# Causal self-attention in a decoder kernel: three score units for two batches instead of four

## What is computed

```
q, k = rope(x @ wq), rope(x @ wk);  v = x @ wv          # 16 heads of 8
s = (q_h . k_h) / sqrt(8), -inf where key > query       # 128 x 128 per batch and head
x = layernorm(x + (softmax(s) @ v_h, heads joined) @ wo)
```

## Time and profile before

| | us |
|---|---|
| median of 3 runs | 1953.66 (1953.19 to 1954.66) |
| the profiled execution's own span | 1948.6 |
| what lies around the span (median minus span) | 5.1 |
| the self-attention block within the span | 0 to about 309.4 |
| one group in its middle, from `a_Y` to `a_Y` | 34.9 |

### The profile page before, as it was taken

One profiled execution on the slowest core, in us unless ns is written; L12 is line 12 of the kernel. 1 busy time (PEld: TensorE's weight loads), 2 busy tenths in 40 slices (PEclk: granted clock), 3 DMA queues, 4 the chain that ended last, 5 costly groups with the idle time before them and its releaser, 6 DMA issues. The chain is left out here.

```text
span 1948.6 us, 31799 instructions
## 1 busy us (share of the span) xinstructions
PE 1562.9 (80%) x10219; PEld 1017.4 (52%) x10219; DVE 1491.3 (77%) x2947; ACT 953.5 (49%) x1491; POOL 920.7 (47%) x938
## 2 busy tenths in 40 slices
PE   8889888989699978977878878769998811699991
PEld 4545547988476632322333333236776611588891
DVE  6899986887488779999989999967777678533335
ACT  3545543575544567657656666436566410011114
POOL 4455442444200147677676677654344100366653
PEclk8999998999899989999988999979999855799996
DMA  4000000000000000000000000020000040466654
GB/s 144 2 0 0 0 1 27 2 2 1 12 1 0 1 1 1 1 1 0 0 1 0 0 0 1 1 78 11 5 9 5 3 145 0 159 209 206 212 171 135
DMA packets 49075, 75.34 MB, mean 39 GB/s; under 512 B 8861, under 2 KB 34821, under 8 KB 48437
## 3 DMA queue, kind: packets, MB, share of 16 engines
q1 hardware_dynamic: 43541, 64.12, 10.5%
q0 software_dynamic: 4544, 9.32, 1.6%
q10 hardware_dynamic: 864, 0.33, 0.1%
HBM read 62.26 MB, written 11.48 MB: 38 GB/s over the span
## 5 line engine op out<-in xcount | busy, mean ns | idle before, releaser
L1506 POOL TENSOR_TENSOR m_hC<-m_h,m_Cs 128x512 f32<-128x512 f32 x256 | 328.2, 1287 | 169.2 <-DVE m_h L1680 122.6
L1788 PE MATMUL PS<-m_hC,identf 128*128 128x512 f32 x512 | 296.5, 662 | 100.9 <-POOL m_hC L1506 99.9
L1680 DVE TENSOR_TENSOR_SCAN m_h<-m_dA,PS 128x512 f32<-128x512 f32 x256 | 312.4, 1220 | 11.2
L1788 PEld LDWEIGHTS PS<-m_hC,identf 128*128 128x128 f32 x512 | 93.0, 203 | 236.4 <-POOL m_hC L1506 208.9
L1675 DVE TENSOR_TENSOR PS<-PS,m_DU 128x512 f32<-128x512 f32 x256 | 178.4, 697 | 19.9 <-issue 3.8
L1616 ACT ACTIVATE m_dA<-m_DT,m_A 128x508 f32<-128x508 f32 x256 | 174.3, 714 | 31.3 <-DVE m_DT L1664 31.1
L1996 ACT ACTIVATE e_Sg<-PS 128x512 f32<-128x512 f32 x71 | 42.4, 597 | 223.0 <-PE PS L2238 178.8
L2238 PE MATMUL PS<-e_xT,e_WT 128*128 128x128 f32 x1136 | 143.8, 281 | 4.9 <-DVE e_xT L2146 3.4
L1608 ACT COPY m_Cs<-PS 128x512 f32<-128x512 f32 x128 | 73.7, 576 | 143.7 <-PE PS L1766 143.5
L2238 PEld LDWEIGHTS PS<-e_xT,e_WT 128*128 128x128 f32 x1136 | 135.4, 195 | 9.3 <-DVE e_xT L2146 7.1
L1935 POOL DMA_INDIRECT e_XG<-token_rows,e_ids x71 | 68.8, 969 | 138.9 <-DVE e_ids L2140 117.6
(11 more groups left out here) (411 smaller groups left out, 3801.6 us busy)
## 6 DMA issues: line engine op xcount, KB each, us to landing
e_WT<-in_w_wgu SPq DMA_DIRECT2D x71, 512.0 KB
token_rows<-X SPq DMA_DIRECT2D x2, 2048.0 KB
e_Y<-expert_rows SPq DMA_DIRECT2D x16, 256.0 KB, 4.0
k_BD<-in_w_bcr SPq DMA_DIRECT2D x1, 2464.0 KB, 9.5
e_w_wd<-in_w_wd SPq DMA_DIRECT2D x1, 2048.0 KB, 7.9
out_dram<-X SPq DMA_DIRECT2D x8, 256.0 KB, 2.4
X<-in_x SPq DMA_DIRECT2D x1, 1792.0 KB, 8.7
x_Cs<-in_ctx SPq DMA_DIRECT2D x8, 154.0 KB
```

The lines of the kernel that those rows point to most:

```text
L1506: nc.gpsimd.tensor_tensor(hC[:, i % ND, :], hst[:, i % ND, :], Cs[:, n % ND, :], ALU.mult).then_inc(s["hC"], 1)
L1680: nc.vector.tensor_tensor_scan(hst[:, i % ND, :], dA[:, i % NA].rearrange("p b l -> p (b l)"), bank(4), 0.0, ALU.mult, ALU.add).then_inc(s ...
L1788: nc.tensor.matmul(bank(5 + ch), c.identf[:, :], hC[:, i % ND, :], start=False, stop=(n == NS - 1)).then_inc(s["yacc"], 1)
```

## The change

The self-attention gets a function of its own, `causal_attention`; `attention` stays for the cross call. Two batches (a **pair**, e = 0, 1) now share the 128 lanes: batch e has lanes 64e to 64e+63. A pair has UP = 3 units. Units 0 and 1 hold the queries 64 to 127 of both batches, 8 heads x 128 keys each. Unit 2 (EARLY) holds the queries 0 to 63 of both batches, 16 heads x 64 keys. So a group has UN = 6 units, each of the same 128 x 1024 elements as before. What follows from it:

- A late unit's scores are four matmuls with 64-column weights (two row groups x two column groups) of 512 columns, and the mask is 64 keys wide: two matmuls of 4 x 64 columns.
- An early unit is scored in two halves (`early_half`, `score_rest`), each four matmuls and two masks of 256 columns. The second waits for the first (semaphore `lo`) and stands one step later in PE's order.
- Outputs are made once a pair: for each batch 16 matmuls for the late and 8 for the early queries, all over 64 moving columns.
- The early queries need the values of keys 0 to 63 in another layout, `a_VL`: 8 more small matmuls a group (`project_early_values`), two more ACT copies of 64 partitions, and in the prelude a POOL memset of 128 x 3072.
- PE's stream is unrolled over the groups; the other engines keep the loop.

```diff
+    UP = 3
+    UN = PAIRS * UP
+    EARLY = 2
+    VL = sb("VL", [P, 2, GB * 4, VE])
...
+            def early_values(g, par, at=AUX):
+                act.wait_ge(s["ep"], g + 1)
+                for hp in (0, 1):
+                    r = slice(HQ * hp, HQ * hp + HQ)
+                    nc.scalar.copy(VL[r, par].rearrange("p m (j c) -> p m j c", c=32 + 2 * DH)[:, :, :, hp * DH:(hp + 1) * DH],
...
+            def body(g, par, left):
+                if left:
+                    rotate(g + 1, 1)
+                for u in range(2, UN - 1):
+                    less_max(g, u + 1)
+                    sums(g, par, u)
+                    if left and u < 4:
+                        rotate(g + 1, u)
+                sums(g, par, UN - 1)
...
+            def block_of(par, b, gp, out, queries, keys, start):
+                r = slice(32 * gp, 32 * gp + 32)
+                nc.tensor.matmul(out, QM[r, par, b * P + queries:b * P + queries + HQ], BD[r, par, :, b, 0:keys], start=start, stop=False)
...
+            def score(g, par, u):
...
+                if u % UP == EARLY:
+                    early_half(par, pair, at, 0).then_inc(s["lo"], 1)
+                    return
+                for e in (0, 1):
+                    for i in (0, 1):
+                        block_of(par, 2 * pair + e, 2 * (u % UP) + i, PS[HQ * e:HQ * e + HQ, at + i, :], HQ, P, True)
+                for i in (0, 1):
+                    ins = masked(PS[:, at + i, :].rearrange("p (j k) -> p j k", j=HG)[:, :, HQ:P])
+                ins.then_inc(s["s_ready"], 1)
...
+            def early_half(par, pair, at, lo):
+
+                cols = slice(lo * HG * HQ, (lo + 1) * HG * HQ)
+                for e in (0, 1):
+                    for i in (0, 1):
+                        block_of(par, 2 * pair + e, 2 * i + lo, PS[HQ * e:HQ * e + HQ, at + i, cols], 0, HQ, True)
+                for i in (0, 1):
+                    ins = masked(PS[:, at + i, cols])
+                return ins
...
+                for e in (0, 1):
+                    b, lanes = 2 * pair + e, slice(HQ * e, HQ * e + HQ)
+                    for j in range(HG):
+                        for gp in range(4):
+                            nc.tensor.matmul(PS[32 * gp:32 * gp + 32, OUT, columns(pair, 1, e)], V[:, par, b * 4 + gp, 32 * j:32 * j + 32],
+                                             PT[:, UP * pair + gp // 2, gp % 2 * HG + j, lanes], start=(j == 0), stop=(j == HG - 1))
+                    for j in (0, 1):
+                        for gp in range(4):
+                            ins = nc.tensor.matmul(PS[32 * gp:32 * gp + 32, OUT, columns(pair, 0, e)], VL[:, par, b * 4 + gp, 32 * j:32 * j + 32],
+                                                   PT[:, UP * pair + EARLY, gp * 2 + j, lanes], start=(j == 0), stop=(j == 1))
```

More of the change, by code:

```diff
@@ L2267, in plan_weights @@
         1: {"wq": [D, D], "wqp": [D, D], "wk": [D, D], "wkp": [D, D], "wv": [D, D], "wo": [D, D],
-            "cos": [D, P], "sin": [D, P], "hmask": [D, 4], "cmask": ([P, P], BF16)},
+            "cos": [D, P], "sin": [D, P], "hmask": [D, 4], "cmask": ([P, P // 2], BF16)},
         2: {"wq1": [D, D], "wkv1": [D, 2, D], "wo1": [D, 2, 2, D], "wq2": [D, D], "wkv2": [D, 2, D], "wo2": [D, 2, 2, D],
@@ L2344, in first_pe @@
             pe.wait_ge(s_identity, 16)
-        attention(c, "a_", False, Ws[1], sem[1], count[1], (s_x, s_rest), {"sp": first_sp, "act": first_act, "dve": first_dve, "pe": first_pe})
+        causal_attention(c, Ws[1], sem[1], count[1], (s_x, s_rest), {"sp": first_sp, "act": first_act, "dve": first_dve, "pe": first_pe})
         if UPTO >= 2:
@@ L2382, in layout @@
     w["w1_hmask"] = (np.arange(D)[:, None] % 32 // 8 == np.arange(4)[None, :]).astype(f)
-    w["w1_cmask"] = np.where(np.arange(P)[None, :] > np.arange(P)[:, None], -BIG, 0.0).astype(bf)
+    w["w1_cmask"] = np.where(np.arange(P // 2)[None, :] > np.arange(P)[:, None] % (P // 2), -BIG, 0.0).astype(bf)
     order = np.array([4 * (i % 2) + i // 2 for i in range(8)])
```

359 lines of the change are left out of this document (added).

## The result

The changed kernel takes 1919.28 us (median of 4 runs, 1917.47 to 1920.89) against 1954.16 us for the kernel before in the same session (1953.19 to 1958.92). The ratio is 0.9818, with a 95% interval from 0.9805 to 0.9831. The profiled executions agree: 1915.6 us of span where it was 1948.6. The medians give -34.9 us, the spans -33.0. Forecast were 1917.4 us and -36.3.

What follows compares the result with a forecast made beforehand. DVE and PE share the bound, PE longer after the change; legs of 11.84 and 18.79 us make a period of 30.6 instead of 34.9. Savings 4.0 + 6 x 4.3 + 6.5 = 36.3 give 1917.4 us, range 1900 to 1942.

Steps and rivals of the forecast that it cites:

- The case as worked out: Whole kernel: a middle group's period of 30.6 us, off by up to 1 us, 1909 to 1928 us; chance 0.64.
- cheaper outputs: Rival on PE's output matmuls: 13 ns a record, 2.3 us a group saved, about 1900 us in all; chance 0.08.
- the clock: Rival: PE's waits gather in one leg and its clock falls, some 3 us a group, 1940 us; chance 0.07.
- if PEclk drops in the middle groups: One of three listed signs, in the middle groups' PE clock, that would make the prediction wrong.
- DVE leg: Middle group, from the start of `a_Y` to unit 3's transposes: 11.84 us, with PE waiting about 3.
- PE leg: Middle group, from unit 3's transposes through `wo` to the next `a_Y`: 18.79 us, PE running without a wait.
- The rival by which column groups take turns: Score matmuls on the same row groups run one after another: 3.0 us more a group, 1941 us; chance 0.12.
- I take 25 ns, since the loads don't shrink: Price of each of a pair's 96 output records on PE: 2.45 us a pair instead of 2.02.
- PEclk 1.00 in the middle: Expected sign: PE's granted clock stays at 1.00 in the middle groups.
- -6.5: Last group of the block: 27.4 us instead of 33.9.
- some 2: Last group: microseconds added to a walk of 25 because PE falls to 1.2 GHz there.
- -4.0: Group 0: loses the same work, but its first units run at a lower clock and it has one more score step.

Runs made afterwards that it cites:

- e6_rolled: The changed kernel with PE's stream put back into the hardware loop of two bodies instead of unrolled: 1915.29 us.
- e5_outputs_split: The changed kernel with each output matmul of 64 moving columns split into two of 32, 192 records a pair instead of 96: 1940.95 us.
- e1_fill: The changed kernel with eight spare bf16 matmuls of 512 columns ahead of unit 3's transposes in each group but the last: 1906.90 us.
- e2_fill_last: The changed kernel with spare matmuls before unit 3's transposes and, in the last group, before the transposes of units 2 to 5 and the reciprocals: 1904.72 us.
- e3_norm_late: The changed kernel with DVE's norm of a group moved into the next group's body, behind the sum of unit 4: 1900.81 us.
- e10_fold_after_norm: The changed kernel with POOL adding the rotated keys before the fold of unit 2 instead of behind it: 1906.26 us.

## Why the prediction was right, and where it only came out right

The median, 1919.28, lies 1.9 us from the forecast. That is luck in good part, for three steps were off and cancelled: outputs priced too dear (some 12 us in the middle groups), no fall of the clock there (8 us the other way), and a last group priced 5.4 us too short. The case as worked out, with 0.64, did not come; two of its rivals came together, cheaper outputs (0.08) and the clock (0.07), with opposite signs. And by the prediction's own list, "if PEclk drops in the middle groups", it was wrong there.

**Right as worked out.** The period is the sum of a DVE leg and a PE leg. The DVE leg was forecast at 11.84 and is 11.93. DVE's busy time was forecast at 26.0, and is 25.9 to 26.0. The score tiles of 32 x 64 overlap fully: 1.02 to the mask (forecast 1.10), an early half 0.59 (forecast 0.65). The rival by which column groups take turns is gone, and the rule of the Trainium skill, page "TensorE: Matmul & The Clock Gate", section on packing small matmuls, doesn't hold for these tiles: four tiles on two row groups have all eight loads in by 0.21 us while the matmuls run. PE is the longer leg, 16.8 against 11.9. POOL's memset costs 2.66 us under the loads, and unrolling costs nothing: `e6_rolled` shows it, and the changed kernel has 18 instruction packets in 61 to 250 us without a gap on PE. One reading was off without harm: in the earlier trace rows the four loads have begun by 0.2 us, but their busy time goes on to 0.30.

**"I take 25 ns, since the loads don't shrink".** This term of PE's sum was mis-sized. A pair's outputs take 1.48 us instead of 2.45, near the lower bound, and that is the rival of cheaper outputs. `e5_outputs_split` shows that it is mostly columns that are paid for, and the loads kept pace. This is -1.9 us a group; with other small terms the PE leg at full clock is 16.8 instead of 18.8.

**The clock.** "PEclk 1.00 in the middle" was wrong in five groups of six. The prediction had it as a rival with 0.07. The mechanism was the rival's (the waits gather in one leg and the largest is 2 us), and the size half of its 3 us: +1.6 a group. `e1_fill` shows it by taking it away. In the kernel before, PE's waits for the exponentials went up to 1.21 us in the middle groups, and the clock stayed at 1.00. Together with the outputs the middle groups come to -4.9 each instead of -4.3.

**The last group, "-6.5".** Its walk gave 24.9 us at full speed, and 27.4 with the clock (the text says "some 2", the sum has 2.5). That share for the clock is what failed. Between the transposes of unit 3 and the end, the steps on the path take, by the timelines above and those of the middle group:

- transposes and last scores 5.19 instead of 2.8, +2.4;
- behind them, ACT's exponentials of the last unit stand in its queue behind the copy of unit 4's transposes, and these on PE behind the first pair's outputs. From the last scores to the transposes' end is 253.00 + 1.97 - 250.28 = 4.7 us, where full speed has 1.48 + 1.04 = 2.5: +2.2 for the clock, and the queue itself makes the exponentials 0.9 later, which the walk didn't see;
- reciprocals +0.5, the second pair's outputs 2.6 instead of 1.5 (2.45 forecast), `wo` 2.1 instead of 1.2.

That is some 7 us for the clock. It fits the 25.8 left of `e2_fill_last`. The fills themselves took only 1.8 us off against `e1_fill`, because they stand on the same path; where in the group the clock falls is worth another 1.9, as the runs without a fill there show.

**Group 0, "-4.0".** It gained 6.3. Its two pairs of outputs, 1.9 us cheaper at full clock, would account for most of the difference. The rest is within the prelude's own spread. It wasn't tested apart.

## What to carry to other kernels

When two engines hand work back and forth once a round, the period is the sum of the stretches in which each is ahead of the other, not the larger busy time. Work taken out of one such stretch counts only by what it has beyond the wait that it had covered: the norm's 2.2 us freed 0.8, and a wait of 1.2 came to light. When a change gathers TensorE's small waits into one, look at its granted clock behind the gap and price the chain at 1.2 GHz where nothing runs beside it; here filling the gap with matmuls that compute nothing gave 8 us in the middle groups, and on the last group's path 1.8 us in one kernel and nothing in another. And look for a DVE instruction that is long in one place and short in another: it may be standing behind GpSimd.

## What was not expected of the hardware

- The clock fell behind waits of about 2 us in five groups and not behind the third's of 2.07, in both profiles of this kernel. It did not fall behind waits of 1.28 (`e3_norm_late`, `e10_fold_after_norm`). The length of the wait alone doesn't decide it, and what spares a group is open: in `e6_rolled` waits of 1.85 and 2.00 were spared and waits of 1.86 and 1.97 were not. The last group's length moves by 1.9 us with the place where the clock falls.
- One f32 instruction of 128x128 on DVE took 1414 ns instead of 337 beside GpSimd's 128x512 addition, in the kernel before (1418) as in the changed one.
- Output matmuls on four column groups cost 15 ns a record with 64 columns and 9 ns with 32, though one load goes with each. Before, the same with 128 columns took 1.01 us for 32 records.
- Bursts of 192 short matmul records brought gaps of up to 3.1 us in which PE had nothing to wait for, worse in a loop than unrolled. All 15 end 2.1 to 2.9 us after a packet of the instruction queue starts.
